# First cross attention: stacks prepared during the context split, first queries loaded by ScalarE

## The reference, cut to what matters

```python
x = x + L0_xattn(layernorm(x), ctx, w_qkv, w_proj, b_proj)   # 16 heads of 8; keys: 1601 of the context and 256 own
x = x + L0_ffn(layernorm(x), ...)
x = x + L1_xattn(ctx, layernorm(x), mask, b)                 # 8 heads of 16; keys: 1601 of the context, masked
x = x + L1_ffn(layernorm(x), ...)
...                                                          # L2 and L3, not touched
```

## Time and profile before

| | us |
|---|---|
| median of three runs | 4383.67 |
| span of the profiled execution | 4381.2 |
| TensorE busy in it | 3735.4 (85%) |
| VectorE busy | 2959.0 (68%) |
| ScalarE busy | 2383.6 (54%) |
| GpSimd busy | 1543.0 (35%) |
| `cross0`: first load of context to first score | 10.73 to 198.92 |
| `cross0`: attention, first to last maximum begun | 199.6 to 897.2 |
| `cross1`: GpSimd's first fill to first score | 1222.33 to 1285.26 |

### The profile page before, as it was taken

One profiled execution on the slowest core, in us unless ns is written; L12 is line 12 of the kernel. 1 busy time (PEld: TensorE's weight loads), 2 busy tenths in 40 slices (PEclk: granted clock), 3 DMA queues, 4 the chain that ended last, 5 costly groups with the idle time before them and its releaser, 6 DMA issues. The chain is left out here.

```text
span 4381.2 us, 72541 instructions
## 1 busy us (share of the span) xinstructions
PE 3735.4 (85%) x28025; PEld 2217.6 (51%) x28030; DVE 2959.0 (68%) x4913; ACT 2383.6 (54%) x4244; POOL 1543.0 (35%) x1271
## 2 busy tenths in 40 slices
PE   3299999989829997699779999999999999999654
PEld 2133333358703333467446666666666666666442
DVE  3399999944427773655437777777777777777747
ACT  3188888853319896222216656666656566666330
POOL 0200000000040000322006667766666777676410
PEclk6599999989959998799789999999999999999877
DMA  5322222100044540000010000000000000000000
GB/s 174 67 45 45 51 49 48 31 17 17 13 72 77 82 63 2 29 2 2 9 60 1 16 1 16 1 16 1 16 1 16 1 16 1 1 1 1 7 30 24
DMA packets 119911, 123.02 MB, mean 28 GB/s; under 512 B 21200, under 2 KB 97840, under 8 KB 119184
## 3 DMA queue, kind: packets, MB, share of 16 engines
q1 hardware_dynamic: 119432, 117.95, 12.2%
q10 hardware_dynamic: 144, 0.52, 0.0%
HBM read 102.56 MB, written 15.73 MB: 27 GB/s over the span
## 5 line engine op out<-in xcount | busy, mean ns | idle before, releaser
L831 DVE TENSOR_REDUCE att_peak.1<-psS 128x1 f32<-128x512 f32 (+1 forms) x1024 | 580.3, 631 | 95.7 <-PE psS L701 95.6
L2191 POOL TENSOR_TENSOR key_sums_0.1<-key_sums_0.1,prob_0.1 128x512 f32<-128x512 f32 x256 | 440.4, 1720 | 28.7 <-POOL key_sums_0.1 L2191 0.4
L2191 POOL TENSOR_TENSOR key_sums_1.1<-key_sums_1.1,prob_1.1 128x512 f32<-128x512 f32 x256 | 420.1, 1641 | 28.7 <-POOL key_sums_1.1 L2186 0.4
L800 ACT ACTIVATE att_probT.1<-psT 128x512 f32<-128x512 f32 (+1 forms) x682 | 368.7, 568 | 75.0 <-PE psT L730 33.5
L831 DVE TENSOR_REDUCE att_peak.2<-psS 128x1 f32<-128x512 f32 (+1 forms) x512 | 266.5, 568 | 139.6 <-PE psS L701 137.9
L2100 DVE TENSOR_TENSOR att_highest.1<-att_highest.1,prob_0.1 128x1024 f32<-128x1024 f32 (+1 forms) x160 | 273.2, 1708 | 128.3 <-ACT prob_0.1 L2035 121.3
L2100 DVE TENSOR_TENSOR att_highest.1<-att_highest.1,prob_1.1 128x1024 f32<-128x1024 f32 (+1 forms) x160 | 279.3, 1745 | 114.5 <-ACT prob_1.1 L2035 107.7
L701 PE MATMUL psS<-key_stack.1,query_stack.1 64*128 64x512 bf16 (+1 forms) x1024 | 271.6, 386 | 94.8 <-DMA key_stack.1<-key_parts 48.2
L747 PE MATMUL psM<-att_probT.1,quad_values.1 128*9 128x256 f32 (+1 forms) x3840 | 306.3, 391 | 19.5 <-issue 19.5
L2121 DVE TENSOR_TENSOR prob_0.1<-prob_0.1,psO 128x1024 f32<-128x1024 f32 (+1 forms) x256 | 243.7, 1013 | 49.0 <-PE psO L1951 49.0
L2121 DVE TENSOR_TENSOR prob_1.1<-prob_1.1,psO 128x1024 f32<-128x1024 f32 (+1 forms) x256 | 243.7, 1013 | 49.1 <-PE psO L1951 49.1
(11 more groups left out here) (696 smaller groups left out, 8070.2 us busy)
## 6 DMA issues: line engine op xcount, KB each, us to landing
key_stack.1<-key_parts SPq DMA_DIRECT2D x384, 58.0 KB
key_stack.2<-key_parts SPq DMA_DIRECT2D x96, 200.1 KB
ctx_rows.1<-in_ctx_dram SPq DMA_DIRECT2D x8, 1536.0 KB
key_parts<-split_parts.1 SPq DMA_DIRECT2D x8, 1200.8 KB, 5.6
ctx_keys_0.1<-in_ctx_dram SPq DMA_DIRECT2D x4, 768.0 KB
ctx_keys_1.1<-in_ctx_dram SPq DMA_DIRECT2D x4, 768.0 KB
query_stack.1<-query_parts SPq DMA_DIRECT2D x192, 16.0 KB
ctx_values_0.1<-in_ctx_dram SPq DMA_DIRECT2D x4, 768.0 KB
```

The costliest lines, as they stand in the source:

```text
L800: last = self.k.nc.scalar.activation(probs[:, blks[0]:blks[-1] + 1, :].rearrange("p b q -> p (b q)"), bank[0:w, 0:len(blks) * S], ACT.Exp)
L831: self.k.nc.vector.tensor_reduce(self.peak[:, 2 * h + s, c:c + 1], self.score_bank[m % 3][:, 0:w], AX_X, ALU.max).then_inc(self.peak_done. ...
L2191: nc.gpsimd.tensor_tensor(acc, acc, own[:, h, c * BANK:(c + 1) * BANK], ALU.add).then_inc(self.summed.sem, 1)
```

## The change

Three things change. The tiles that GpSimd fills are placed in the scope of the whole `cross0` (`early`), and the other tiles of the attention by a new method `open` later. `split_context` takes a function, `prepare`, and runs it on GpSimd; `cross0` gives it `pool_prepare`. And the first 12 query loads are issued by ScalarE, at the head of `act_run`, after the same wait for `zeroed`; SyncE begins with the keys. The last point holds for `cross1` as well, since it shares the class; there `pool_prepare` stays at the head of the attention block.

```diff
--- before.py
+++ after.py
@@ -361,7 +361,7 @@
             load_context(k, sp, buffers[par], (bp * 2 + par), loaded[par])
 
 
-def split_context(k):
+def split_context(k, prepare):
 
 
     nc = k.nc
@@ -374,6 +374,10 @@
         rest = k.sb("split_rest", [P, 2, KC], ctx=mem)
         parts = k.sb("split_parts", [P, 2, 3, KC], BF16, ctx=mem)
         block = mem.enter_context(nc.Block())
+
+        @block.gpsimd
+        def _(pool):
+            prepare(pool)
 
         @block.sync
         def _(sp):
@@ -456,7 +460,7 @@
     SCORE_SLOTS = {8: [[(1, 3)], [(1, 4)], [(1, 5)], [(1, 6)], [(1, 7)], [(2, 0)], [(2, 1)], [(2, 2)]],
                    7: [[(1, 3), (1, 4)], [(1, 5)], [(1, 6)], [(1, 7)], [(2, 0)], [(2, 1)], [(2, 2)]]}
 
-    def __init__(self, k, mem, chunks, blocks, bins, hd, heads, halves, masked=False):
+    def __init__(self, k, early, chunks, blocks, bins, hd, heads, halves, masked=False):
         self.k, self.chunks, self.blocks, self.bins, self.hd, self.heads = k, chunks, blocks, bins, hd, heads
         self.halves, self.masked = halves, masked
         self.pairs = B * heads // 2
@@ -467,18 +471,12 @@
         self.score_slots = self.SCORE_SLOTS[self.NB]
         sb = k.sb
...
-        self.key_stack = sb("key_stack", [P, self.RING, 2, *lanes, self.width], BF16, ctx=mem)
-        self.query_stack = sb("query_stack", [P, 2, 4, *lanes, S], BF16, ctx=mem)
+        self.key_stack = sb("key_stack", [P, self.RING, 2, *lanes, self.width], BF16, ctx=early)
+        self.query_stack = sb("query_stack", [P, 2, 4, *lanes, S], BF16, ctx=early)
         if masked:
-            self.bias = sb("att_key_bias", [P, 2, self.NK], ctx=mem)
-        self.ident = sb("ident_bf16", [P, P], BF16, ctx=mem)
-        self.peak = sb("att_peak", [P, 4, self.NC], ctx=mem)
-        self.shift = sb("att_shift", [P, 4], ctx=mem)
-        self.shift_parts = sb("att_shift_parts", [P, 4, 3], BF16, ctx=mem)
-        self.probT = sb("att_probT", [P, self.RING, 2, self.NK, S], ctx=mem)
-        self.vquad = sb("quad_values", [P, 2, self.NK, 4, hd + 1], ctx=mem)
-        self.sums = sb("att_sums", [P, S], ctx=mem)
-        self.rtotal = sb("att_rtotal", [P, 2, 4], ctx=mem)
+            self.bias = sb("att_key_bias", [P, 2, self.NK], ctx=early)
+        self.ident = sb("ident_bf16", [P, P], BF16, ctx=early)
+        self.vquad = sb("quad_values", [P, 2, self.NK, 4, hd + 1], ctx=early)
         self.score_bank = [k.psS[:, n, :] for n in range(3)]
         self.key_bank = [k.psS[:, 3, :], k.psT[:, 0, :], k.psT[:, 1, :]]
         self.partial = k.psM[:, 0:S]
@@ -495,6 +493,16 @@
         self.queries_loaded = [k.flag(f"queries_loaded_{i}") for i in range(2)]
         self.ctx_loaded = [k.flag(f"ctx_loaded_{i}") for i in range(2)]
         self.bias_loaded = [k.flag(f"mask_loaded_{i}") for i in range(2)] if masked else None
+
+    def open(self, mem):
+
+        sb = self.k.sb
+        self.peak = sb("att_peak", [P, 4, self.NC], ctx=mem)
+        self.shift = sb("att_shift", [P, 4], ctx=mem)
+        self.shift_parts = sb("att_shift_parts", [P, 4, 3], BF16, ctx=mem)
+        self.probT = sb("att_probT", [P, self.RING, 2, self.NK, S], ctx=mem)
+        self.sums = sb("att_sums", [P, S], ctx=mem)
+        self.rtotal = sb("att_rtotal", [P, 2, 4], ctx=mem)
 
     def finish(self):
         pairs, quads = self.pairs, self.quads
@@ -622,7 +630,7 @@
         per = self.heads // 4
         sp.wait_ge(*self.zeroed(self.zeroings))
         for q in range(self.quads):
-            if q % 2 == 0:
+            if q % 2 == 0 and q > 0:
                 self.load_queries(sp, q // 2)
             self.load_keys(sp, q)
             if q == 0:
@@ -675,7 +683,6 @@
             self.k.nc.gpsimd.memset(place if self.halves else place[:, :, h, :], 0.0).then_inc(self.cleared.sem, 1)
 
     def pool_run(self, pool, crows, own=None):
-        self.pool_prepare(pool)
         for q in range(self.quads + 2):
             if q < self.quads:
                 self.pool_stage(pool, crows, own, q)
@@ -810,6 +817,8 @@
         self.k.nc.scalar.copy(self.sums[:], self.partial).then_inc(self.partial_copied.sem, 1)
 
     def act_run(self, act):
+        act.wait_ge(*self.zeroed(self.zeroings))
+        self.load_queries(act, 0)
         for g in range(-1, self.pairs + 2):
             q, odd = divmod(g, 2)
             for i in range(self.NB):
@@ -874,10 +883,14 @@
     nc = k.nc
     H, hd = 16, 8
     NKEY = KC + S
-    split_context(k)
+    chunks = [(0, 512), (512, 512), (1024, 512), (1536, KTAIL + S)]
+    blocks = [(t * P, P) for t in range(KB - 1)] + [((KB - 1) * P, KTAIL), (KC, P), (KC + P, P)]
+    bins = [(t, t + 1) for t in range(0, KB - 1, 2)] + [(KB - 1,), (KB, KB + 1)]
     own_done, own_copied = k.flag("value_done"), k.flag("value_copied")
     att_turned, att_copied, proj_done = k.flag("att_turned"), k.flag("att_copied"), k.flag("proj_done")
     with ExitStack() as mem:
+        att = PairedAttention(k, mem, chunks, blocks, bins, hd, H, halves=True)
+        split_context(k, att.pool_prepare)
         wqkv = k.sb("wqkv", [P, 3, P], ctx=mem)
         wproj = k.sb("wproj", [P, P], ctx=mem)
         wT = k.sb("wT", [P, 4, P], ctx=mem)
@@ -914,12 +927,9 @@
                 nc.vector.tensor_copy(vself[:].rearrange("p t d -> p (t d)"), banks).then_inc(own_copied.sem, 1)
         own_done.passed(1)
         own_copied.passed(1)
-        chunks = [(0, 512), (512, 512), (1024, 512), (1536, KTAIL + S)]
-        blocks = [(t * P, P) for t in range(KB - 1)] + [((KB - 1) * P, KTAIL), (KC, P), (KC + P, P)]
-        bins = [(t, t + 1) for t in range(0, KB - 1, 2)] + [(KB - 1,), (KB, KB + 1)]
         with ExitStack() as own:
             crows = [k.sb(f"ctx_values_{i}", [P, KB, D], ctx=own) for i in range(2)]
-            att = PairedAttention(k, own, chunks, blocks, bins, hd, H, halves=True)
+            att.open(own)
             block = own.enter_context(nc.Block())
 
             @block.sync
@@ -1044,6 +1054,7 @@
         blocks = [(t * P, P) for t in range(KB - 1)] + [((KB - 1) * P, KTAIL)]
         bins = [(t, t + 1) for t in range(0, KB - 1, 2)] + [(KB - 1,)]
         att = PairedAttention(k, mem, chunks, blocks, bins, hd, H, halves=False, masked=True)
+        att.open(mem)
         block = mem.enter_context(nc.Block())
 
         @block.sync
@@ -1052,6 +1063,7 @@
 
         @block.gpsimd
         def _(pool):
+            att.pool_prepare(pool)
             att.pool_run(pool, crows)
 
         @block.tensor
```

## The result

The changed kernel takes 4349.92 us, the median of four runs (4348.34 to 4354.48), against 4383.82 for the kernel before in the same comparison (4382.56 to 4385.84): 33.9 us less, a ratio of 0.9927 with a 95% interval of 0.9915 to 0.9939. The forecast was 4344.5, a gain of 39.2, with a range of its own from 4341 to 4349 and a wider one from 4340 to 4356; the result lies in the wider one and 0.9 us above the narrow one. The profiled span falls from 4381.2 to 4347.6 us, by 33.6.

What follows compares the result with a forecast made beforehand. The prediction took the first attention's start as bound by GpSimd's fills for 31 us, then by loads for 14.4. Gains of 34.7 + 4.5 = 39.2 us took 4383.7 to 4344.5 us; range 4340 to 4356.

Steps and rivals of the forecast that it cites:

- The fills, 31.2 us: First attention's start: moving GpSimd's fills into the split removes SyncE's wait of 31.2 us, so loads issue at 153.3.
- Hidden by the block of the split: Context split: 31.06 us of GpSimd fills fit inside its 81.1 us block, ending near 41.8, 50 us before the barrier.
- No cost to the split's chain: Context split: the fills slow no link of its chain of loads, casts and subtractions; taken as nothing.
- The rival of blocking: Context split: fills hold up VectorE's L430 by 8.9 and 3.0 us, some 12 us lost, 4356.5; chance 0.08.
- The query loads, 3.5 + 4.5 us: Starts of both attentions: ScalarE issues queries beside SyncE's keys, saving 4.14 less 0.6 us, then 5.7 less 1.2.
- what the two sets of transfers take from each other: First attention's start: queries moving beside keys delay the keys by 0 to 1.2 us; the middle, 0.6, was taken.
- Nothing was put ahead: Behind the first keys: each later load keeps its distance to them, so the whole stage shifts.
- The forecast's own sign of being wrong: First attention: a first score later than 166, expected near 164.2, would show the prediction wrong.
- From there on the same distances to the end: From the second attention's first score, expected at 1246.1, everything to the end keeps its distances.
- the clock rival: Long later stage, 2300 to 4100: TensorE's granted clock falling to 0.978 loses 39 us, to 0.96 gives 4415; chance 0.02.
- Issues of two engines one after the other: Both attentions' starts: ScalarE and SyncE cannot issue side by side, only 31.2 us stay, 4352.5; chance 0.12.
- No gain: First attention's start: something else held SyncE at 153.3, so the time stays 4383.7; chance 0.02.

Runs made afterwards that it cites:

- the kernel with both attentions' fills hidden: Changed kernel plus first attention's first loads a block earlier and second attention's fills, as 4-byte elements, in the three blocks ahead of its own: 4311.51 us.
- rest held back: Changed kernel, but SyncE, after the first quad's keys, waits until the first queries have landed before issuing context values and all that follows: 4350.51 us.

## Why the prediction was right, and which term was mis-sized

**The fills, 31.2 us: right.** The issues moved from 184.50 to 153.68, by 30.8; the block started 0.4 later. The fills' move alone gives 4350.7 us against 4349.9 for the whole change, and the query loads' move alone gives nothing that can be told from no change.

**Hidden by the block of the split: right.** The fills beside it cost nothing while they end inside it, and 16.1 us of them appear when 16 us stick out.

**No cost to the split's chain: right.** The rival of blocking expected L430 to wait 8.9 and 3.0 us. It did not wait. What set it apart is the kind of operation. TENSOR_TENSOR with two on-chip inputs is untouched by a fill (1.83 us beside bf16 fills, 1.82 beside float32 ones) and slowed by up to 0.8 us by GpSimd's reads; TENSOR_SCALAR and CAST are held until the running fill ends. One input alone is not the mark: 16 BATCH_NORM_STATS2 took 3.19 us beside the fills of the kernel with both attentions' fills hidden, as without any.

**The query loads, 3.5 + 4.5 us: the failed term.** In the first attention it measured -1.5 and in the second +2.1, so 0.6 in place of 8.0; this 7.4 is more than the 5.3 us by which the gain fell short of the forecast. The total came closer than the mechanism did, by 2.2 us that unchanged code happened to give in the profiled execution; that part is luck. The step that failed is the one on "what the two sets of transfers take from each other", put at 0.6 us. It rested on "nearly the same for very different sizes, so this is time of the issuing engine and not of the transfer". That is true of the issues and says nothing about the end of the loads. The keys' own transfers take 3.9 us of the set at a share of at most 0.56, 7 us, and were not done when their issues were; the queries' transfers, 1.6 us of the set at about 0.56, are worth 2.8 by this estimate and not 0.6. The runs bound that only roughly: from their own first issue to the first score the keys took 10.3 us before, 9.5 with the fills alone and 12.0 behind queries that had landed, and 12.7 and 12.9 with queries beside them. Of the 4.1 us of issue time saved ahead of the keys there is little left by that: with all else held back the start takes 12.7 us, with one queue 13.6. The 0.65 us that I read for the queries came from a stretch in which they ran alone (0.74 in the experiment that runs them alone), and beside keys they take twice that.

**"Nothing was put ahead": wrong.** Nothing was put ahead of the keys. The queries, though, used to stand ahead of all else in SyncE's queue and were complete before the keys were. On their own queue they compete with keys, context values and next keys, and land last. The forecast's own sign of being wrong, a first score later than 166, came true with 169.59. This competition is the other 3.2 us, shown by holding the rest back. Why, in the first attention, queries on ScalarE's queue are hurt by that company, and keys on it are not (12.9 us), stays open; the two differ in the size of their packets (0.20 MB in 480 against 0.71 MB in 288), and no run varied that alone.

**"From there on the same distances to the end": not quite, and the clock rival came true in small.** The gain was 32.2 us at the second attention's first score, 39.0 at the layer norm of `cross3` (2262.3 before, 2223.3 now), 30.8 at the next layer norm, behind that stage's attention (4120.5 and 4089.7), and 33.6 at the end. So code that did not change gave 6.8 us on the way to `cross3`, and between that stage's two layer norms the changed kernel lost 8.2 us, again in code that did not change, as much as all that the query loads could have given. The windows of the whole stretch, and of its first 70 us, show where. The kernel before:

```profile
2262.30:4120.50 1858.20, 1809.19 (x12384) 1205.14 (x12384) 1389.10 (x1228) 1104.72 (x1583) 1270.89 (x896) 0.99 0.03 10
...
2262.30:2332.30 70.00, 49.93 (x257) 31.97 (x258) 34.33 (x67) 32.90 (x51) 10.54 (x8) 0.83 0.28 94
```

The changed kernel:

```profile
2223.30:4089.70 1866.40, 1818.08 (x12384) 1209.36 (x12384) 1389.93 (x1229) 1104.21 (x1583) 1270.58 (x896) 0.99 0.03 10
...
2223.30:2293.30 70.00, 51.27 (x234) 31.49 (x236) 30.53 (x65) 26.93 (x42) 4.85 (x4) 0.73 0.29 94
```

The same 12384 products keep TensorE busy for 8.9 us longer, and the granted clock is lower at the start: from 30 to 40 us into the stretch the kernel before is at 1.00, the level of 2.4 GHz, and the changed one still at 0.50, the level of 1.2 GHz. As an estimate, 0.83 - 0.73 over 70 us is 7.0 us of work at full clock, and a dip to 0.83 from 80 to 90 us, which the kernel before does not have, another 1.7. The mean over the whole stretch, 0.99 in all profiles, is too coarse to show it. The 14 profiled executions of this document fall in line:

| profiled executions | clock granted in the first 70 us | length of the stretch |
|---|---|---|
| kernel before and five experiments | 0.83 to 0.85 | 1858.0 to 1858.9 |
| six experiments | 0.76 to 0.78 | 1861.3 to 1863.1 |
| changed kernel, rest held back | 0.73, 0.71 | 1866.4, 1866.9 |

What makes the clock rise earlier or later there is open; each kernel has one profile, so it is not shown to belong to the change.

**The rivals.** Issues of two engines one after the other: did not happen (4.15 and 4.39 us side by side), though the time came out between it (4352.5) and the forecast, for another reason. Fills blocking VectorE: not here, as above. The clock: 1.00 through the middle of the long late stage, as before, and not the 39 us that this rival priced; but at the start of that stage it cost 8 us in the profiled execution. No gain: excluded by the interval.

## What to carry to other kernels

Work of an idle engine that prepares data was free in an earlier block as long as it ended inside it and the other engines' operations there were not of a kind that it shuts out; look at the kind first, and cut long fills into pieces where they are. Before moving loads to another engine's queue to save issue time, compare the issue time with the time until the last byte lands: if the loads are bound by transfer the issue time is not what the move saves, and it gives up the order in which the loads would have landed. Here it lost 1.7 and 2.3 us where loads of 8 rows kept the DMA share near one half, and won 1.5 and 2.7 with loads of 16 rows. Starting such loads a block earlier gained what moving them did not. And where a total does not add up from the seams, look at the granted clock in the first windows of the unchanged stages, not only at its mean.

## What the runs showed of the hardware that I had not expected

- A fill takes time by elements and not by bytes: the same 38 KB of each partition took 16.11 us as 19212 bf16 zeros in the kernel before and 8.11 us as 9612 float32 zeros.
- A GpSimd fill held VectorE's TENSOR_SCALAR for 7.7 and 7.9 us, and left a two-input operation beside it at 1.83. Cut into pieces of 1.6 and 1.8 us, it still cost each TENSOR_SCALAR and CAST beside it 1.0 to 2.1 us.
- Adding a second quad's keys to keys and queries left the DMA share at 0.53 to 0.56; adding context values took it to 1.16.
- The queries' packets took 0.74 us of the set alone, and 1.6 beside the keys.
- The length of one unchanged stretch, 1858.0 to 1866.9 us, went with the clock granted in its first 70 us, 0.85 to 0.71.
